# Causal attention: value products of two key tiles issued together, a ring of four steps of exponentials, and plain maxima of two heads in one VectorE instruction

## The reference, cut to what matters

```
k = jnp.repeat(k, groups, axis=2)          # groups = 4: four query heads share one key head
v = jnp.repeat(v, groups, axis=2)
scores = jnp.einsum('bqhd,bkhd->bhqk', q, k) * scale
causal = jnp.tril(jnp.ones((S, S), dtype=bool))
scores = jnp.where(causal[None, None], scores, jnp.finfo(scores.dtype).min)
probs = jax.nn.softmax(scores, axis=-1)
attn = jnp.einsum('bhqk,bkhd->bqhd', probs, v).reshape(B, S, NH * HD)
```

## Time and profile before

| | |
|---|---|
| median of 3 runs | 1742.45 us (1739.26 to 1745.59) |
| the profiled execution: span from its first to its last instruction | 1739.7 us |
| causal attention, from the first to the last value product | 358 us to 1219 us of the span |
| busy over the whole span: PE, DVE, ACT, POOL | 1630.1, 1173.3, 946.3, 556.3 us |

### The profile page before, as it was taken

How to read it: one execution, slowest core, us unless ns; L and a number is a source line. 1 busy time by engine, 2 the same in 40 slices (tenths; PEclk the granted TensorE clock), 3 DMA queues, 4 the chain that set the end, 5 groups by cost and what they waited for, 6 DMA issues and landing times. The chain is left out here.

```text
span 1739.7 us, 29572 instructions
## 1 busy us (share of the span) xinstructions
PE 1630.1 (94%) x9040; PEld 804.0 (46%) x9040; DVE 1173.3 (67%) x3195; ACT 946.3 (54%) x2069; POOL 556.3 (32%) x842
## 2 busy tenths in 40 slices
PE   7799998899999999999999999998895899999996
PEld 3367665333333333333333333332784455555564
DVE  6632788799888888888888888880685334434342
ACT  6034554256677676776767767677574233333332
POOL 3441238073515003030030300000277344444443
PEclk9899998799999999999999999999996899999999
DMA  5000000311030300303003030000378677777774
GB/s 164 0 7 19 1 2 7 61 26 38 1 62 2 59 4 1 62 2 59 5 1 62 2 61 3 2 1 1 99 238 286 117 130 129 130 129 129 132 125 71
DMA packets 252194, 105.76 MB, mean 61 GB/s; under 512 B 208064, under 2 KB 247880, under 8 KB 252040
## 3 DMA queue, kind: packets, MB, share of 16 engines
q1 hardware_dynamic: 233296, 80.62, 21.8%
q0 software_dynamic: 13392, 18.49, 6.3%
q10 hardware_dynamic: 5352, 4.76, 0.8%
HBM read 30.88 MB, written 23.67 MB: 31 GB/s over the span
## 5 line engine op out<-in xcount | busy, mean ns | idle before, releaser
L1674 ACT ACTIVATE prob<-pS 128x512 f32<-128x512 f32 (+3 forms) x1280 | 597.1, 534 | 256.3 <-PE pS L1562 134.1
L1731 DVE TENSOR_REDUCE mx<-pM 128x1 f32<-128x512 f32 x768 | 503.1, 686 | 70.3 <-PE pM L1542 66.5
L1542 PE MATMUL pM<-KT,QT 96*128 96x512 bf16 (+3 forms) x1280 | 444.1, 357 | 8.7 <-DMA QT<-Qt 4.6
L1558 PE MATMUL pS<-QT,KT 99*128 99x512 bf16 (+3 forms) x1280 | 416.5, 350 | 3.7 <-ACT prob L1674 2.8
L1577 PE MATMUL pO<-prob,VV 128*32 128x512 f32 (+3 forms) x2560 | 299.9, 540 | 14.6 <-ACT prob L1674 14.3
L2437 PE MATMUL bank<-w13T,QKV 128*128 x568 | 257.8, 598 | 16.5 <-ACT QKV L2464 16.5
L1727 DVE CUSTOM_DVE_ANT_0 junk<-pM,mask_row 128x128 bf16<-128x128 f32 (+3 forms) x512 | 241.6, 484 | 46.3 <-PE pM L1542 42.9
L1542 PEld LDWEIGHTS pM<-KT,QT 96*128 96x128 bf16 x1280 | 124.2, 98 | 268.5 <-DVE mx L1731 109.9
L1467 POOL CAST mpart<-mneg 128x16 bf16<-128x16 f32 x32 | 6.8, 211 | 663.2 <-DVE mneg L1739 663.2
L2497 DVE TENSOR_TENSOR QKV<-QKV,bank 128x512 f32<-128x512 f32 x71 | 48.9, 688 | 234.3 <-issue 199.1
L1558 PEld LDWEIGHTS pS<-QT,KT 99*128 99x128 bf16 x1280 | 123.6, 98 | 143.0 <-ACT prob L1674 79.8
(11 more groups left out here) (356 smaller groups left out, 1954.6 us busy)
## 6 DMA issues: line engine op xcount, KB each, us to landing
raw<-in_ffn_w_dram SPq DMA_DIRECT2D x48, 256.0 KB, 3.6
QKV<-queue SPq DMA_DIRECT2D x71, 136.0 KB, 2.6
out_dram<-x ACTq DMA_DIRECT2D x8, 512.0 KB, 4.7
x<-_attn_hidden_states_dram SPq DMA_DIRECT2D x14, 256.0 KB, 5.9
QKV<-QKV SPq DMA_TRANSPOSE x142, 3.3
QT<-mrow SPq DMA_DIRECT2D x128, 3.0 KB
out_dram<-QKV POOLq DMA_INDIRECT x71, 3.9
wc_s<-in_attn_Wc_dram SPq DMA_DIRECT2D x1, 1024.0 KB, 7.9
```

The source lines that it names most:

```text
L1542: last = nc.tensor.matmul(pM[:, bank, 0:w], QT[0:ROWS, par, h, qt * P:(qt + 1) * P], KT[0:ROWS, par, 512 * part:512 * part + w], start=Tru ...
L1558: last = nc.tensor.matmul(pS[:, p % NSC, lo:512], KT[0:ROWS + 3, par, kt * P:(kt + 1) * P], QT[0:ROWS + 3, par, h, 512 * c + lo:512 * c + ...
L1674: nc.scalar.activation(prob[:, n % 3, h, lo:512], pS[:, p % NSC, lo:512], ACT.Exp, scale=SCALE).then_inc(s.head_exp, 1)
L1731: nc.vector.reduce_max(mx[:, h, qt, part:part + 1], pM[:, plan.bank[item], 0:w], AX.X).then_inc(s.unit_max, 1)
```

## The change

Four things are changed. First, `values` of two steps are issued one behind the other, in every even step, and `prob` has four steps instead of three (`RING`). Second, plain maxima of two heads become one item `("V", gi, pr, qt, part)`: two products into two neighbouring banks of `pM`, one semaphore, and one VectorE instruction over both banks, which writes two columns of `mx`. A `V` begins at an even bank; where the next bank is odd, that one is passed over. Third, the order of the items: heads go in pairs, query tiles inside, and `M` is put 7 items later instead of 10; the planner prices a `V` at 2 * 512 + 110. Fourth, SBUF space for the larger ring: the routing tables of the next stage, `maskf` and `stats` are allocated later or laid into other tiles.

```diff
+RING = 4
@@ def background
-            items += [("U", gi, h, qt, part) for h in range(GRP) for qt in range(4 * c, 4 * c + 4) for part in range(c + 1)]
+            for pr in range(GRP // 2):
+                for qt in range(4 * c, 4 * c + 4):
+                    items += [("V", gi, pr, qt, part) for part in range(c)]
+                    items += [("U", gi, 2 * pr + n, qt, c) for n in range(2)]
             items.append(("M", CH * gi + c))
...
-        items.insert(at + 10, items.pop(at))
+        items.insert(at + 7, items.pop(at))
@@ def cost
+    if item[0] == "V":
+        return 2 * 512 + 110
@@ class Plan
+        free = 0
+        for item in order:
+            by = {"M": "mrow_out", "U": "unit_max", "V": "unit_max", "O": "o_put"}[item[0]]
+            wide = 2 if item[0] == "V" else 1
+            if wide == 2 and free % 2:
+                free += 1
+            bank = free % BANKS
+            free += wide
...
@@ tensor
+                    if kind == "V":
+                        for n in range(2):
+                            last = nc.tensor.matmul(pM[:, bank + n, :], QT[0:ROWS, par, 2 * h + n, qt * P:(qt + 1) * P],
+                                                    KT[0:ROWS, par, 512 * part:512 * part + 512], start=True, stop=True)
+                        last.then_inc(s.unit_mm, 1)
+                        return
...
-                                                prob[:, n % 3, h, lo:512], start=(kt == 0),
+                                                prob[:, n % RING, h, lo:512], start=(kt == 0),
...
-                    if n:
+                    if n % 2 == 0 and n:
+                        values(n - 2)
                         values(n - 1)
...
+                values(last_step - 1)
                 values(last_step)
@@ scalar
-                    if n >= 3 and h == 0:
-                        act.wait_ge(s.pv, n - 2)
+                    if n >= RING and h == 0:
+                        act.wait_ge(s.pv, n - RING + 1)
@@ vector
+                    if item[0] == "V":
+                        nc.vector.tensor_reduce(mx[:, 2 * h:2 * h + 2, qt, part],
+                                                pM[:, plan.bank[item]:plan.bank[item] + 2, :], AX.X,
+                                                ALU.max).then_inc(s.unit_max, 1)
+                        return
...
-                        nc.vector.reduce_max(mx[:, h, qt, part:part + 1], pM[:, plan.bank[item], 0:w],
-                                             AX.X).then_inc(s.unit_max, 1)
@@ SBUF
-        maskf = sb("maskf", [P, P], F32, ctx)
-        prob = sb("prob6", [P, 3, GRP, 512], F32, ctx)
+        prob = sb("prob6", [P, RING, GRP, 512], F32, ctx)
-        stats = sb("stats5", [P, T, 6], F32, ctx)
+        maskf = byc_pool[:, 0:P]
+        stats = room[:, 1664:1664 + 6 * T].rearrange("p (t k) -> p t k", k=6)
```

More of the change, by code:

```diff
@@ L1108, in stages_layer2 @@
         woT, gwT = v.woT, v.gwT
-        pad_at = sb("pad_at", [P, E], I32, late)
         mv5 = sb("mv5", [P, T, 2], F32, late)
         norm1 = sb("norm1", [P, 3, T], F32, late)
[L1112 to L1117, removed]
         queue = nc.dram_tensor("queue", [E * CAP + P, REC], F32).ap()
@@ L1124, in stages_layer2 @@
             w2T = sb("w2T", [P, FFN // P, E * H], F32, att)
+            pad_at = sb("pad_at", [P, E], I32, att)
+            jrow_i = sb("jrow_i", [P, NTAB], I32, att)
+            jrow, ej, before, rowf = (sb(n, [P, NTAB], F32, att) for n in ("jrow", "ej", "before", "rowf"))
+            steps = sb("steps", [P, T], F32, att)
+            padf, ntile, ends = (sb(n, [P, E], F32, att) for n in ("padf", "ntile", "ends"))
+            counts = sb("counts", [P, E], F32, att)
+            tile_expert, tile_in = (sb(n, [P, NTAB], I32, att) for n in ("tile_expert", "tile_in"))
             stage7(nc, sb, ps, sem, locals(), v)
@@ L1240, in __init__ @@
         last = [None] * BANKS
-        for n, item in enumerate(order):
-            by = {"M": "mrow_out", "U": "unit_max", "O": "o_put"}[item[0]]
-            counts[by] += 1
-            self.bank[item], self.clear[item], self.count[item] = n % BANKS, last[n % BANKS], counts[by]
-            last[n % BANKS] = (by, counts[by])
-        self.units_through = {}
+        free = 0
[6 more added lines that the diff above has]
+            free += wide
+            counts[by] += 1
+            self.bank[item], self.count[item] = bank, counts[by]
+            before = [x for x in last[bank:bank + wide] if x]
+            self.clear[item] = [(name, max(k for n, k in before if n == name)) for name in sorted({n for n, _ in before})]
+            last[bank:bank + wide] = [(by, counts[by])] * wide
+        self.last_unit = {}
         for k in range(CH * NG):
-            self.units_through[k] = max(self.count[x] for x in order if x[0] == "U" and CH * x[1] + x[3] // 4 == k)
-        self.last_unit = {x: CH * x[1] + x[3] // 4 for x in order
-                          if x[0] == "U" and self.count[x] == self.units_through[CH * x[1] + x[3] // 4]}
+            units_of = [x for x in order if x[0] in "UV" and CH * x[1] + x[3] // 4 == k]
+            self.last_unit[max(units_of, key=lambda x: self.count[x])] = k
 def stage6(nc, sb, ps, sem, env, base_env):
@@ L1391, in _ @@
                 nc.gpsimd.memset(VV[:, :, :, HD:HD + 1], 1.0).then_inc(s.vv_init, 1)
-                nc.gpsimd.memset(maskf[:, :], 0.0).then_inc(s.zero, 1)
+                nc.gpsimd.memset(maskf, 0.0).then_inc(s.zero, 1)
                 pool.wait_ge(s.zero, 3)
-                nc.gpsimd.affine_select(out=maskf[:, :], in_=maskf[:, :], compare_op=ALU.is_ge, fill=NEG, base=0,
+                nc.gpsimd.affine_select(out=maskf, in_=maskf, compare_op=ALU.is_ge, fill=NEG, base=0,
                                         pattern=[[1, P]], channel_multiplier=-1).then_inc(s.masks, 1)
                 pool.wait_ge(s.masks, 2)
-                nc.gpsimd.tensor_copy(mask_kq[:, :], maskf[:, :]).then_inc(s.masks_b, 1)
+                nc.gpsimd.tensor_copy(mask_kq[:, :], maskf).then_inc(s.masks_b, 1)
                 pool.wait_ge(s.masks_b, 2)
@@ L1519, in take @@
                 def take(item):
-                    if plan.clear[item] is not None:
-                        name, count = plan.clear[item]
+                    for name, count in plan.clear[item]:
                         pe.wait_ge(s[name], count)
@@ L1716, in beside @@
                 def beside(item):
-                    if item[0] != "U":
+                    if item[0] == "M":
                         return
@@ L1720, in beside @@
                     dve.wait_ge(s.unit_mm, plan.count[item])
-                    w = unit_width(qt, part)
[L1722 to L1729, removed]
-                    else:
-                        nc.vector.reduce_max(mx[:, h, qt, part:part + 1], pM[:, plan.bank[item], 0:w],
-                                             AX.X).then_inc(s.unit_max, 1)
+                    if item[0] == "V":
[3 more added lines that the diff above has]
+                        return
+                    w = unit_width(qt, part)
+                    if plan.count[item] <= 2:
+                        dve.wait_ge(s.masks, 1)
+                    else:
+                        dve.wait_ge(s.unit_max, plan.count[item] - 2)
+                    nc.vector.tensor_tensor_reduce(junk[:, plan.count[item] % 2, 0:w], pM[:, plan.bank[item], 0:w],
+                                                   mask_row[:, 512 - w:512], 1.0, -3e38, ALU.add, ALU.max,
+                                                   mx[:, h, qt, part:part + 1]).then_inc(s.unit_max, 1)
                     if item in plan.last_unit:
```

2 lines of the change are left out of this document (1 added, 1 removed).

## The result

The changed kernel takes 1819.4 us (median of 4 runs, 1818.7 to 1820.1), the kernel before 1741.2 beside it: a ratio of 1.0454, 95% interval 1.044 to 1.0468. It is 78 us slower, where 1744 us was forecast, and lies outside the range of 1720 to 1768.

A forecast was written before the change was run, and what follows sets the result against it. TensorE's order was taken as the steady bound, narrowly over VectorE, which bounds the first 62 us. Steady groups -2, group starts -6, end +3, beginning +5, skipped banks +2 gave +2 us: 1744 us, range 1720 to 1768.

The forecast's parts named there:

- Value products together: TensorE's value blocks in attention: one entry and exit saved per two steps, 0.18 us each, 3.6 us per group.
- The wait of 0.92 us at a group's start: Value block waiting for ScalarE at a group's start: forecast to go, -6 us over 7 groups.
- close behind: ScalarE's three banks around a double block: up to 5.64 us per two steps, hidden under VectorE's 5.9.
- Plain maxima in pairs: VectorE's maxima in attention: a pair costs 1.13 us instead of 1.20, saving 3.4 us of VectorE per group.
- what is queued behind: Readers behind TensorE's double block: VectorE idles 1.2 us per full double; 3.3 us new waits per group against 3.6 won.
- stay near TensorE's bound: Double steps with a narrow tile: shorter block or fewer items, eleven per group at about 0.1 us over TensorE's bound.
- The beginning: First 62 us of attention, where VectorE is full: forced idle outweighs the pairs' saving, 62 to some 67 us, +5.
- The order, the ring, the rest: Prob ring, item order, M, skipped banks, SBUF moves: -6 us at group starts, +2 for skipped banks, otherwise 0.
- VectorE starves: Rival: behind each double block VectorE idles 1.5 us per full double; 1774 us, from 1757 on; chance 0.25.
- Its sign: Test for the starving rival: it decides once VectorE's mean idle per double block passes 1.2 us.
- The merge saves nothing: Rival: the second value block pays TensorE's 0.09 and 0.54 us again; 1760 us; chance 0.07.
- the saving lands: Rival: VectorE's forced idle is nearer 0.8 us, TensorE stays the bound; 1715 us, up to 1733; chance 0.26.

The follow-up runs named there:

- the singles: The changed kernel with each plain maximum single and M 10 items later, keeping double value blocks and the new head order: 1736.3 us, ratio 0.9981 to the kernel before.
- The ladder: Series of kernels with double blocks that adds, to single maxima at 1736.3 us, what a pair consists of, up to the changed kernel at 1819.4 us.
- the plan in pairs with M at 7: Double blocks, items planned as pairs (price 1134, M 7 later), then taken apart into single maxima spread over a step's five places: 1756.0 us, ratio 1.009.
- M and the price: Against the singles: M 7 items later instead of 10 and a plain product priced 567 instead of 622: 1751.4 us, ratio 1.0056.
- side by side in one place: Changed kernel with two 512-column reductions per pair, each bank ready and freed by itself, pairs beginning at any bank: 1778.9 us, ratio 1.022.
- even banks: Changed kernel with two reductions per pair, each bank ready and freed by itself, but pairs beginning only at even banks: 1780.9 us, ratio 1.0227.
- free together: Changed kernel with two reductions per pair and a signal after each product, but both banks waited for and freed together: 1807.3 us, ratio 1.0392.
- ready together: Changed kernel with two reductions per pair, one signal behind the second product, both banks freed after the second reduction: 1831.0 us, ratio 1.0519.
- one instruction for two: The changed kernel itself, one 1024-column reduction per pair instead of two of 512: 1819.4 us, ratio 1.0454 to the kernel before.
- short reductions: Changed kernel with each pair's reduction over 64 of 512 columns per head and the exponentials' scale a tenth: 1727.8 us, ratio 0.9933.

## Why the prediction was wrong

*Value products together.* Right in the mechanism and in the size of the block: 1.86 us, and two steps at the end 5.2. The end takes 4.6 us more where 3 were forecast; some 1.3 of them are the lower clock, for which the forecast had no term. The wait of 0.92 us at a group's start is gone: the block at 729.03 has none. But the gain is smaller: in the singles a group is 2.0 us shorter, where the forecast had 3.6 and the 0.9 of that wait. ScalarE, which I had named as standing "close behind" VectorE's wait, holds it back there.

*Plain maxima in pairs.* The size was right (1.14 us per pair). The step that failed is the next one, *what is queued behind*. Its first half held: the forecast was 1.2 us of idle behind a full double block and 0.95 behind an average one, 19 us for the 20 of a group; measured are 1.23 at the place shown and 17.1 in the group. Its second half did not. I let VectorE lose time only behind double blocks, and took the later of two engines in each double step: 3.3 us of new waits in a group against 3.6 won. The runs show a group 8.0 us longer, so 11.5 us of new waits if the 3.6 are counted as won, three times as much. The missing part can be seen from two sides.

By place, it is idle time between the blocks, which the forecast put at nothing: 8.0 us of the group, 2.4 before. It is the pair ring by itself, which I had priced at 0.07 us won per pair. Pairs with single blocks cost 47 us; by my reckoning, with a block of 1.09 us, VectorE would have been idle 2.35 - 2.11 = 0.24 us per block there. I had reckoned with a ring always full of 2.27 us of work. A pair behind two narrow masked items has 0.4 to 0.7 us of work before it and is ready 0.6 us after its start, with both banks waited for first.

By double step, it is those with a narrow tile, which should "stay near TensorE's bound". From one block's start to the next, the nine doubles of full width take 5.96 us on average (5.9 was forecast, 5.48 in the singles); the eleven with a narrow tile take 5.70, against 5.19 in the singles and in the kernel before. More than half of what a group lost against the singles, 5.5 of 9.9 us, is there.

*The ladder*, from 1736 (singles, double blocks) up: the plan in pairs with M at 7 +20, of them M and the price 15; side by side in one place +23; even banks +2; free together +26; ready together +24; one instruction for two -12: 1819.

*The beginning.* +5 was forecast for the first 62 us, which are the first 20 steps; they take 71.3 instead of 62.1, +9. The whole first group is 13.5 us longer.

*The order, the ring, the rest.* Skipped banks +2, as taken, though 35 and not 64. "`M` 7 items later is some two steps, as 10 items were", and that POOL "is no wait", held as to the wait and was wrong as to the cost: 9 us with single maxima.

*The rivals.* "VectorE starves" is what happened, at its place and beyond: 1819 against 1774. I gave it 0.25, since I had bounded it with the double block alone. Its sign, a mean idle of over 1.2 us per double block, did not come: it is 0.86 (17.1 over 20 blocks). The forecast's idle behind blocks was about right, and the loss beyond it came from where it had none. "The merge saves nothing" and "the saving lands" are both out: the first by the 1.86 us block, the second by the result.

Left open: why moving M by some items costs 9 us, and how the 32 us that pairs and double blocks cost beyond their sum divide among the rungs, which were all climbed with double blocks.

## What to carry to other kernels

A larger instruction saves its fixed cost, here 0.07 us of 1.2, but it can also make the buffer ring coarser: ask what the ring holds in the worst mix of items, not when full, and count when the first half becomes ready and the last half free. Where an engine with an in-order queue fills small rings for two readers, lumps in its order can cost time even though every engine has slack over the stage. VectorE's busy time fell by 24 us here (1173.3 to 1148.9), and the kernel became 78 us longer. Try each half of a double edit alone before measuring both.

## What the runs showed that was not expected

An edit can be harmless alone and not beside another: double value blocks alone left the time as it was (0.9984), with pairs they cost some 32 us. VectorE's work in a group could fall from 92 to 49 us (singles against short reductions) with the group at 106.4 and 106.7: there VectorE's load did not set the time. In the singles the exponentials did in part (103.2 with half of them); for the short reductions that was not tested.
